# A key or value projection ahead of the weighted value products in TensorE's order, on one Trainium2 core

## The reference

```python
q = (query @ wq).reshape(bs, sq, 32, 128)      # query: layer-normed x
k = (key @ wk).reshape(bs, sk, 8, 1, 128)      # key, value: ctx; each of 8 groups serves 4 query heads
v = (value @ wv).reshape(bs, sk, 8, 1, 128)
q, k = rope(q), rope(k)
attn = softmax(q @ k.T / sqrt(128) + mask)
out = (attn @ v) @ wo
x = x + tanh(g_xattn[1]) * out
```

## Time and profile before

| | us |
|---|---|
| median of 3 runs | 873.41 |
| lowest and highest run | 869.49, 873.47 |
| profiled execution, its own time | 871.6 |
| its span, first to last instruction | 869.8 |
| TensorE (PE) busy in the span | 781.7 (90%) |
| VectorE (DVE) busy | 678.1 (78%) |
| ScalarE (ACT) busy | 354.0 (41%) |
| GpSimd (POOL) busy | 364.6 (42%) |

### The profile page before, as it was taken

How to read it: one execution, slowest core, us unless ns; L and a number is a source line. 1 busy time by engine, 2 the same in 40 slices (tenths; PEclk the granted TensorE clock), 3 DMA queues, 4 the chain that set the end, 5 groups by cost and what they waited for, 6 DMA issues and landing times. The chain is left out here.

```text
span 869.8 us, 12638 instructions
## 1 busy us (share of the span) xinstructions
PE 781.7 (90%) x4276; PEld 615.0 (71%) x4276; DVE 678.1 (78%) x1250; ACT 354.0 (41%) x1063; POOL 364.6 (42%) x300
## 2 busy tenths in 40 slices
PE   2899988878799999999999999999999999994674
PEld 1555554766688878888778888878888887763562
DVE  5888887778787787777878777787777777876994
ACT  2777775221233424334243333433433333243552
POOL 2777777215543433224344233343332332203662
PEclk9999999998899999999999999999999999997897
DMA  8310030101021111101121010111111102002001
GB/s 255 98 48 24 24 102 1 37 0 49 19 56 49 42 43 38 36 25 37 37 61 37 25 37 25 49 37 41 46 30 32 37 13 55 1 1 72 13 36 48
DMA packets 37444, 37.41 MB, mean 43 GB/s; under 512 B 2897, under 2 KB 27217, under 8 KB 37393
## 3 DMA queue, kind: packets, MB, share of 16 engines
q1 hardware_dynamic: 35168, 32.81, 12.7%
q10 hardware_dynamic: 2224, 3.94, 1.5%
HBM read 34.64 MB, written 2.10 MB: 42 GB/s over the span
## 5 line engine op out<-in xcount | busy, mean ns | idle before, releaser
L923 POOL TENSOR_TENSOR dense<-rope_a,rope_b 128x512 f32<-128x512 f32 x62 | 79.4, 1281 | 189.1 <-DVE rope_b L1036 189.1
L976 ACT ACTIVATE ot_hi<-PB 128x512 fp32r<-128x512 f32 x64 | 38.4, 600 | 211.3 <-PE PB L1281 211.3
L1195 PE MATMUL QB<-xT_hi,wq_lo 128*128 128x512 f32 x256 | 107.8, 421 | 2.4 <-DVE xT_lo L1109 2.4
L967 ACT ACTIVATE e_sb<-masked,nmax 128x64 f32<-128x64 f32 x256 | 86.5, 340 | 56.0 <-DVE nmax L1065 55.3
L1195 PE MATMUL ROW<-wo_hi,ot_lo 128*128 128x512 f32 x256 | 102.0, 398 | 2.9 <-DVE ot_lo L1083 2.6
L1033 DVE TENSOR_TENSOR rope_a<-QB,rope 128x512 f32<-128x512 f32 x62 | 42.9, 692 | 78.3 <-PE QB L1197 78.1
L1196 PE MATMUL QB<-xT_lo,wq_hi 128*128 128x512 f32 x256 | 102.3, 400 | 0.0
L1197 PE MATMUL QB<-xT_hi,wq_hi 128*128 128x512 f32 x256 | 102.0, 399 | 0.0
L1196 PE MATMUL ROW<-wo_lo,ot_hi 128*128 128x512 f32 x256 | 101.6, 397 | 0.0
L1197 PE MATMUL ROW<-wo_hi,ot_hi 128*128 128x512 f32 x256 | 101.1, 395 | 0.0
L1036 DVE TENSOR_TENSOR rope_b<-QB,rope 64x512 f32<-64x512 f32 x124 | 85.4, 689 | 3.9
(11 more groups left out here) (202 smaller groups left out, 1905.4 us busy)
## 6 DMA issues: line engine op xcount, KB each, us to landing
raw<-in_wq SPq DMA_DIRECT2D x32, 256.0 KB, 2.8
raw<-in_wo SPq DMA_DIRECT2D x32, 256.0 KB, 2.6
ctx_two<-in_ctx SPq DMA_DIRECT2D x16, 256.0 KB, 3.7
x_sb<-in_x SPq DMA_DIRECT2D x8, 256.0 KB, 8.1
ctx_raw<-in_ctxT ACTq DMA_DIRECT2D x1, 2048.0 KB, 12.9
raw<-in_wv SPq DMA_DIRECT2D x8, 256.0 KB, 2.7
raw<-in_wk SPq DMA_DIRECT2D x8, 256.0 KB, 3.0
out<-x_sb SPq DMA_DIRECT2D x8, 256.0 KB, 2.0
```

Of the source, the lines that this page charges most:

```text
L923: nc.gpsimd.tensor_tensor(dst, a, b, ALU.add).then_inc(s_rot, 1)
L967: nc.scalar.activation(e_sb[:, r, :], masked[:, r, :], ACT.Exp, bias=nmax[:, r:r + 1], accum_out=zsum[:, r:r + 1]).then_inc(s_exp, 1)
L1195: nc.tensor.matmul(out, lhs[1], rhs[0], start=first, stop=False)
```

## The change

TensorE issues a step's key or value projection, with its waits, directly behind `outputs(N-2)` and ahead of `weighted(N-1)`. Nothing else differs.

```diff
                     if N >= 2:
                         outputs(N - 2)
-                    if N >= 1:
-                        weighted(N - 1)
                     if n in K_SLOTS and (n != 13 or ahead):
                         K = K_SLOTS.index(n) + 1
                         if K == 2:
...
                         kv_free(gp, n)
                         value(V_NEXT[n])
+                    if N >= 1:
+                        weighted(N - 1)
```

## The result

| | before | changed |
|---|---|---|
| median, runs | 872.57 us, 22 | 875.78 us, 22 |
| lowest and highest | 868.52, 874.17 | 871.69, 877.06 |
| profiled execution, its span | 871.6, 869.8 | 871.7, 869.8 |

The ratio of the times is 1.0031, with a 95% interval from 1.0018 to 1.0044: 0.31% slower, inside the half per cent and with a clear sign. The two profiled executions are equally long, though. That is an accident of one execution (the changed one began its attention loop 3.2 us sooner), and it is why the stages have to be compared, not the spans.

The account below looks back on a forecast made before the run. TensorE at 2.4 GHz was taken as the bound. Value steps +0.5, key steps +0.9 and stalls behind key steps +1.0 summed to +2.4 us, on a median of 873.4 giving 875.8 us, range 869.7 to 879.5.

Parts of the forecast that it names:

- the half per cent: Whole kernel: 4.4 us, about what a measurement can tell from no change; chance 0.88 of staying within it.
- What bounds it: Attention loop: TensorE is the bound, at 2.4 GHz; none of its waits is at the swapped blocks, so none is relieved.
- TensorE's own time, value step: Last outputs matmul to transposes, 26 value steps: 3.29 us becomes 3.31, +0.02 each, +0.5 us in all.
- x: Seam on TensorE from the value projection's last matmul into the weighted products: 0.21 us, bounds 0.12 and 0.32.
- TensorE's own time, key step: Last outputs matmul to transposes, 15 key steps: 4.61 us becomes 4.67, +0.06 each, +0.9 us in all.
- The engines behind it: VectorE, GpSimd, ScalarE after key steps: late ot_lo delays key rotation, k_rot, query rotation and p_sb; transposes stall 0.2 us, +1.0 total.
- the five places: Key steps followed by a step without projection, n = 5 in four pairs and n = 9 in the last: stall 0.2 us each.
- What I costed at nothing: Later v_lo in value steps, outputs reading ot_lo, KV bank asked for about 0.5 us sooner: slack covers them, no cost.
- the dearer seam: Rival, value projection into weighted products: first weighted matmul 0.40 us behind, +4.9 us, 880.7 in all; chance 0.07.
- The late chain: Rival, transposes after five key steps: the 0.73 us delay left comes through each time, 3.7 not 1.0, 878.5; chance 0.06.
- Cheaper seams: Rival, TensorE in the moved steps: value seam 0.12 us, nothing at keys, no stall, -1.8 us, 871.6; chance 0.12.

## Why the prediction was right, and where it was not

875.8 us was forecast and 875.78 measured, and the forecast of a small slowdown within half a per cent was right. The agreement to hundredths is luck: the median of the kernel before was 872.6 over these runs, not the 873.4 I started from, so the step was +3.2 and not +2.4, and its terms were off in both directions.

- **What bounds it**: right. TensorE stays the bound of the loop, and its waits for rotations and for ot_lo are as long as before.
- **TensorE's own time, value step**: x was forecast at 0.21 and is 0.21. The sum gave +0.02 per step; with the value projections alone moved the loop became 0.28 us shorter, -0.01 per step. Forecast +0.5, measured -0.3: hundredths times 26.
- **TensorE's own time, key step**: mis-sized, +0.9 forecast, about +0.1 found. The projection behind a full-array block takes 2.54 us from first to last matmul (705.44 to 707.98), not the 2.57 of the outputs, so from the last outputs matmul to the transposes it is 4.63 (705.21 to 709.84), against 4.61 before; the key steps at n = 1 and 13 even gained 0.01 each. All seams together came to -0.2, where I had +1.4.
- **The engines behind it**: the mechanism was right at every link, and the five places and no others were right. The kernels that move five blocks, or all but these, show it. The size was not: forecast 0.2 each, measured 0.37. I let the query's products start with k_rot's end (S + 4.85, measured S + 4.95, so a signal of 0.10 us was left out), and I did not count that the query follows the transposes 0.05 later after the wait (0.19 instead of 0.14). 5 x 0.37 = 1.9 us instead of 1.0.
- **What I costed at nothing**: value steps, the outputs, the KV bank: right, no new wait anywhere.
- **Missing**: the part behind the loop. I treated everything behind it as fixed, and it grew by 1.9 us, of which 1.5 are seen at one stretch of the lower clock. The sum in the traces is -0.2 + 1.9 + 1.9 = 3.6, the medians say 3.2 with an interval of about 1.6 to 3.8.

So the mechanism at the five places was forecast, and the total was not earned by it: an overestimate of the seams (+1.6) and two underestimates (-0.9 and -1.9) cancelled in part, and the start of 873.4, 0.8 above the later median, made up what was missing. Of the rivals, the dearer seam fell (0.21, not 0.29). By the Trainium skill, "TensorEngine Tiling (Array Packing)", section Key Properties, a change of the tiling mode drains the TensorE; the seam of 0.21 us is shorter than the 0.28 us which the value matmul before it lasts in the profile, so if the array drains there, it does not wait for that recorded end. The late chain costing its whole 0.73 fell too, by half. Cheaper seams were right in sign for the loop.

No kernel that beats the one before came out of it. The four kernels that keep the change in part or whole and have no stall measure 0.9991 to 0.9998, none apart from 1; moving the projections ahead is worth at best 0.2 to 0.3 us of loop.

## What to carry over

When two blocks of the bounding engine are swapped, the engine's own time hardly moves; look instead in the follower's queue for what stands behind the operand that now comes last, and for a shared buffer that carries the lateness on. Find the step with the least slack: 5 of 41 places made the whole difference. And where a later stage runs with a clock that goes up and down, a microsecond added ahead of it is not a microsecond at the end; compare stages between marks, and test a suspicion by putting neutral time in before explaining it by the change.

## What the runs showed that I had not expected

By the traces the cost of time put into the loop is not a line. Added to the kernel before, 0.88, 1.80 and 3.37 us of TensorE work made it 1.2, 3.4 and 3.1 us slower by the medians, with ends of 95.3, 96.7 and 94.8 us against 94.8. It is the ends, one trace for each kernel, that show it: the intervals of the three medians would also hold a cost of just the added work. In the two traces of each of the two kernels the end repeats to 0.15 us (94.83 and 94.78; 96.77 and 96.63), while the stage ahead of step 2 differs by 6.0 us between those of the changed kernel (246.3 and 252.2), which is about what their times differ by (871.7 and 877.4).
